# Partial sums over 3, 4 and 6 channel blocks, eight output tiles evacuated by ScalarE, and a new order of the first and fourth token groups

## What is computed

```python
ek = exp(min(k, 30)); ekv = ek * v
nf, df = scan(a * decay + ekv), scan(b * decay + ek)      # forward in time, per channel
nb, db = the same, backward in time
num = nf + nb - ekv + exp(min(u + k, 30)) * v             # den likewise, without v
y = sigmoid(r) * num / max(den, 1e-8) * (0.8 + 0.2 * tf)
h = silu(y @ rw1.T + rb1); logits = (h @ rw2.T + rb2)[:, :16] + gates
coeff = softmax of the two largest logits, 0 elsewhere
base = y @ W.T + bias
xa = einsum('ni,eri->ner', y, A)                          # 16 experts x rank 16 = 256 columns
out = x + base + einsum('ner,eor->no', xa * coeff, B)
```

## Time and profile before

| | us |
|---|---|
| median of 3 runs | 674.62 (674.05 to 674.89) |
| the profiled execution | 672.5 |
| its span | 670.7 |
| TensorE busy, in the span | 593.9 (89%) |
| VectorE busy | 517.5 (77%) |
| ScalarE busy | 360.1 (54%) |
| GpSimd busy | 367.8 (55%) |

### The profile page before, as it was taken

The page is one execution under the profiler, slowest core; times in us unless marked ns, Lnnn a source line. Parts: engine busy times, 40 slices in busy tenths (PEclk is TensorE's granted clock), DMA queues, the critical chain, the costliest instruction groups (busy, mean ns, idle before and its releaser), DMA issues.

```text
span 670.7 us, 6900 instructions
## 1 busy us (share of the span) xinstructions
PE 593.9 (89%) x2554; PEld 478.4 (71%) x2554; DVE 517.5 (77%) x579; ACT 360.1 (54%) x429; POOL 367.8 (55%) x182
## 2 busy tenths in 40 slices
PE   0153689979999989999999959999999999999997
PEld 0142567758878757888778848888788888888786
DVE  7999999999999999999699989999699322031202
ACT  6788899855854676566456584558455220020100
POOL 1799999868857864666266764585347301000100
PEclk9967789989999999999999979999999999999999
DMA  5324467525755811237231622345231502050112
GB/s 196 125 92 155 145 231 235 165 92 124 191 125 111 232 66 63 95 105 243 78 121 52 216 98 78 110 139 175 79 110 48 156 1 90 5 158 0 34 61 79
DMA packets 33249, 78.45 MB, mean 117 GB/s; under 512 B 4736, under 2 KB 4928, under 8 KB 33216
## 3 DMA queue, kind: packets, MB, share of 16 engines
q1 hardware_dynamic: 30912, 73.82, 33.6%
q0 software_dynamic: 2304, 4.20, 4.2%
HBM read 57.03 MB, written 20.97 MB: 116 GB/s over the span
## 4 chain that ended last, share of the span: by engine, by line
PE 64%; DVE 18%; POOL 6%; ACT 5%; issue 4%; DMA 2%; SPq 0%; DVEq 0%; ACTq 0%; POOLq 0%
PE acc L983 20%; PE acc L984 19%; PE acc L985 19%; DVE mix L769 3%; DVE mix L773 3%; DVE mix L778 3%; DVE mix L800 2%; PE acc L1014 2%; DVE eu L788 2%; PE acc L1015 2%; DVE yr L807 1%; DVE mix L756 1%; PE acc L1052 1%; POOL y_lo L679 1%; DVE xo L821 1%
## 5 line engine op out<-in xcount | busy, mean ns | idle before, releaser
L983 PE MATMUL acc<-y_hi,wa_hi 128*128 128x512 f32 x638 | 258.5, 405 | 54.1 <-POOL y_lo L679 49.3
L984 PE MATMUL acc<-y_lo,wa_hi 128*128 128x512 f32 x638 | 254.3, 399 | 0.0
L985 PE MATMUL acc<-y_hi,wa_lo 128*128 128x512 f32 x638 | 254.0, 398 | 0.0
L983 PEld LDWEIGHTS acc<-y_hi,wa_hi 128*128 128x128 f32 x638 | 123.7, 194 | 86.4 <-POOL y_lo L679 50.7
L985 PEld LDWEIGHTS acc<-y_hi,wa_lo 128*128 128x128 f32 x638 | 123.2, 193 | 26.7
L984 PEld LDWEIGHTS acc<-y_lo,wa_hi 128*128 128x128 f32 x638 | 123.9, 194 | 25.2
L669 POOL TENSOR_TENSOR mix<-mix,kv 128x1024 f32<-128x1024 f32 x30 | 71.9, 2396 | 77.8 <-DVE mix L756 77.8
L821 DVE SCALAR_TENSOR_TENSOR xo<-acc,bias_sb,xo 128x512 f32<-128x512 f32 x64 | 46.8, 735 | 73.9 <-PE acc L985 73.7
L679 POOL TENSOR_TENSOR y_lo<-yr,y_hi 128x1024 fp32r<-128x1024 f32 x31 | 76.4, 2464 | 37.5 <-ACT y_hi L428 37.5
L692 POOL TENSOR_TENSOR wx_lo<-xa,wx_hi 128x512 fp32r<-128x512 f32 x16 | 21.2, 1346 | 119.6 <-ACT wx_hi L516 119.6
L650 POOL TENSOR_TENSOR yr<-mix,yr 128x1024 f32<-128x1024 f32 x31 | 74.2, 2394 | 4.9 <-DVE yr L807 2.7
(11 more groups left out here) (126 smaller groups left out, 702.1 us busy)
## 6 DMA issues: line engine op xcount, KB each, us to landing
...
out<-xo SPq DMA_DIRECT2D x64, 256.0 KB, 3.8
xo<-x_cm SPq DMA_DIRECT2D x64, 256.0 KB, 3.8
out<-xo POOLq DMA_DIRECT2D x16, 256.0 KB, 6.2
...
```

What stands on the lines that cost most here:

```text
L983: nc.tensor.matmul(out_ap, wh, yh, start=start, stop=False)
L984: nc.tensor.matmul(out_ap, wh, yl, start=False, stop=False)
L985: return nc.tensor.matmul(out_ap, wl, yh, start=False, stop=stop)
```

## The change

**Depth.** `part_depth` gives tiles 0 to 4 partial sums over 3 units, tiles 5 to 9 over 4 and tiles 10 to 15 over 6. `base` of groups 0 and 1 does what is left: 5 units for tiles 0 to 4, 4 for tiles 5 to 9, 2 for tiles 10 to 15. The places of `drain_part` move with it.

**Evacuation.** Of groups 0 and 1, tiles j = 4 to 7 are evacuated by ScalarE (`drain`, PSUM plus bias, no x). The x that is missing there is added to `out` by four DMAs from DRAM to DRAM, 512 KB each (`add_x`), issued by GpSimd.

**Order.** In group 0 the base products of tile 0 over units 3 to 6 stand ahead of the wait for unit 7, and tile 2's stand ahead of `turn`. In group 3 `turn` comes ahead of all of tile 2, and VectorE's `routing` and `weigh` come later in its step. In group 4 `low_rank` of units 5 and 6 stands ahead of the wait for unit 7 of its batch (unit 23), and half of tile 1 ahead of `logits`. In group 1 `routing` and `weigh` come earlier. The high and low parts of the last weight chunk (12) come a step earlier or ahead in their step.

```diff
-        part_steps = {4: (0, 0, 2), 5: (2, 5, 7), 6: (7, 10, 12), 7: (12, 15, 16)}
-        def base_from(G):
-            return HALF if G < SPLIT else 0
+        part_steps = {4: (0, 2, 5), 5: (5, 7, 10), 6: (10, 12, 13), 7: (13, 15, 16)}
+        part_depth = [HALF - 1] * 5 + [HALF] * 5 + [HALF + 2] * 6
+        def base_from(G, j=0):
+            return part_depth[G * CB + j] if G < SPLIT else 0
...
-        evacs_at = {(CB + 2, AFTER_FWD): (0, 2), (CB + 2, AFTER_FWD_NUM): (2, 4), (CB + 2, AFTER_BWD_DEN): (4, 5),
+        evacs_at = {(CB + 2, AFTER_RATIO): (0, 2), (CB + 2, AFTER_FWD): (2, 4), (CB + 5, AFTER_FWD): (8, 11),
...
+        drains_at = {(CB + 2, AFTER_EXP_K): (4, 6), (CB + 2, AFTER_INVERSE): (6, 7), (CB + 3, AFTER_HI): (7, 8),
+                     (CB + 5, AFTER_EXP_K): (12, 13), (CB + 5, AFTER_INVERSE): (13, 14), (CB + 6, AFTER_HI): (14, 16)}
+        x_adds_at = {(CB, AFTER_LO): (4, 5), (CB + 1, AFTER_GATE): (5, 6), (CB + 2, AFTER_GATE): (6, 7),
+                     (CB + 2, AFTER_LO): (7, 8)}
...
-        routing_at |= {(first_step(G) + 1, AFTER_FWD_NUM): G for G in (1, 3)}
+        routing_at |= {(first_step(3) + 1, AFTER_BWD_DEN): 3}
...
-        weigh_at |= {(first_step(1) + 1, AFTER_P2): 1, (THIRD, AFTER_BWD_DEN): SPLIT, (first_step(3) + 1, AFTER_BWD_DEN): 3}
+        weigh_at |= {(first_step(1) + 1, AFTER_BWD_DEN): 1, (THIRD, AFTER_BWD_DEN): SPLIT, (first_step(3) + 1, AFTER_SCALE): 3}
...
+            def drain(e):
+                G, j = divmod(e, CB)
+                act.wait_ge(out_done, e + 1)
+                if e < XBUF:
+                    act.wait_ge(part_stored[(e - 2) % PBUF], 16 * (PARTS // PBUF))
+                else:
+                    act.wait_ge(out_added[e % XBUF], 16 * (e // XBUF))
+                nc.scalar.activation(xo[:, e % XBUF, :], acc[:, out_bank(G, j), :], ACT.Identity,
+                                     bias=bias_sb[:, j:j + 1]).then_inc(drained, 1)
...
+            def add_x(j):
+                pool.wait_ge(part_stored[j % PBUF], 16 * ((j + CB) // PBUF + 1))
+                nc.gpsimd.dma_start(out[j], x_cm[j], accum_op=ALU.add,
+                                    max_dma_last_dim=4 * T).then_inc(x_added[j - CB // 2], 16)
...
             for p in range(5, PARTS):
                 pe.wait_ge(part_out, p - 4)
-                for kc in range(HALF):
+                for kc in range(part_depth[p]):
+                    if kc >= part_depth[p - 1]:
+                        unit_in(0, kc)
+                        pe.wait_ge(w_lo_ready, base_chunk[kc] + 1)
                     base_part(p, kc)
...
-                        if kc - LAG >= k0:
-                            if kc - LAG == k0:
-                                bank_in(G, 3)
-                                pe.wait_ge(w_lo_ready, base_chunk[CB - 1] + 1)
-                            base(G, 0, kc - LAG)
-                    for kc in range(CB - LAG, CB):
-                        base(G, 0, kc)
+                        if kc == CB - 2:
+                            bank_in(G, 3)
+                            pe.wait_ge(w_lo_ready, base_chunk[CB - 1] + 1)
+                            for k in range(k0, CB - 1):
+                                base(G, 0, k)
+                    base(G, 0, CB - 1)
...
+                        if G == 4:
+                            for a in range(2):
+                                low_rank(G, a, kc)
                     for a in range(2):
-                        for kc in range(first, CB):
+                        for kc in range(CB if G == 4 else first, CB):
                             low_rank(G, a, kc)
...
+                if G == 4:
+                    bank_in(G, 4)
+                    for kc in range(4):
+                        base(G, 1, kc)
                 if G != 1:
                     logits(G)
...
-                ahead = {0: CB, SPLIT: CB - 1, 3: 3}.get(G, k0)
+                ahead = {0: CB - 1, SPLIT: CB - 1}.get(G, k2)
```

More of the change, by code:

```diff
@@ L213, in quarter, with drained_by_act, evacuations, x_loads_to @@
             return tasks_at.get(s, (-1, -1))
+        def drained_by_act(e):
+            return e < PARTS and e % CB >= CB // 2
+        def evacuations(e):
+            return sum(1 for i in range(e + 1) if drained_by_act(i) == drained_by_act(e))
+        def x_loads_to(e):
+            return sum(1 for i in range(e + 1) if not drained_by_act(i) and i % XBUF == e % XBUF)
         def held(g):
@@ L233, in decay_mix_with_routed_lora_channel_major @@
         part_out = sem("part_out")
+        x_added = [sem(f"x_added{j}") for j in range(CB // 2)]
+        drained = sem("drained")
         out_added = [sem(f"out_added{i}") for i in range(XBUF)]
@@ L400, in _ @@
                     load_x(e)
+            for j in range(CB // 2):
+                sp.wait_ge(x_added[j], 16)
             for i in range(XBUF):
@@ L579, in _ @@
                     scale_end_den(s)
-                if routed and G != 4:
+                if routed and G not in (3, 4):
                     exp_gap(G)
@@ L598, in _ @@
                         drain_part(p)
-                if routed:
+                if routed and G not in (0, 3):
                     split_wx(G)
@@ L718, in _ @@
                     split_wx(SPLIT)
+                for j in tiles(x_adds_at, s, AFTER_GATE):
+                    add_x(j)
                 for e in tiles(adds_at, s, AFTER_GATE):
@@ L724, in _ @@
                     split_lo(s - 1)
+                for j in tiles(x_adds_at, s, AFTER_LO):
+                    add_x(j)
                 for e in tiles(adds_at, s, AFTER_LO):
@@ L728, in _ @@
                     weights_lo(n)
-                if q == 1 and G != SPLIT:
+                if q == 1 and G not in (SPLIT, 3):
                     split_wx(G)
@@ L732, in _ @@
                     p1(s + 1)
+                if q == 1 and G == 3:
+                    split_wx(G)
                 if s == CB - 2:
@@ L1078, in unit_in @@
                     pe.wait_ge(lo_ready, g + 1)
-            for kc in range(HALF):
+            for kc in range(part_depth[0]):
                 unit_in(0, kc)
@@ L1187, in _ @@
                     pe.wait_ge(wx_ready, 2 * G + a + 1)
-                    for kc in range(k0, k0 + first):
+                    for kc in depths(G, 3 + a)[:first]:
                         base(G, 3 + a, kc)
@@ L1195, in _ @@
                 for j in range(3, 5):
-                    for kc in range(k0 + first, k0 + 4):
+                    for kc in depths(G, j)[first:]:
                         base(G, j, kc)
```

71 lines of the change are left out of this document (44 added, 27 removed).

## The result

The changed kernel takes **679.25 us** (median of 6 runs, 678.56 to 679.59) where the kernel before took 673.95 in the same comparison (672.86 to 674.89). That is 5.3 us more; the ratio, which is formed from the runs beside each other, is **1.0077** (95% interval 1.0064 to 1.0090). The forecast was 677.2 (+2.6 us), in the range 670.5 to 681.5. The direction and most of the mechanism held; the loss is twice the size.

A forecast was written before the change was run, and what follows sets the result against it. TensorE and VectorE were taken to bound different stages, with no TensorE idle time behind its wait for unit 23. +9.3 us before unit 15 and -6.7 behind it gave +2.6, from 674.62 to 677.2 us, range 670.5 to 681.5.

The forecast's parts named there:

- what the deep sums do first: Unit 5 to `hidden(0)`: TensorE waits some 9 us for unit 5, VectorE 7.6 at `inverse(6)`; `hidden` shifts by +13.1 us.
- from `hid` to `weigh(0)`: Group 0: a 3.5 us wait at `logits`, more matmuls and a clock restart add +1.5 us (0.5 to 2.8).
- Other parts of this stretch cost nothing that I can see.: Before unit 15: four `add_x` take GpSimd about 1 us each, within its idle time, so no cost.
- rival of the accumulating DMAs: Steps 10 and 11: ScalarE's `drain(6)` waits for an `add_x` to land, costing VectorE 3 to 4 us: 681; chance 0.15.
- a sign of being wrong: Steps 10 and 11: a ScalarE wait on `out<-xo` of over 2 us would show the forecast wrong.
- the wait for `logits(1)`: Group 1: VectorE reaches `routing(1)` at 197.0, TensorE starts `logits(1)` at 199.0; VectorE waits 3.0 us.
- The gains of 5.5 and 2.8: Before unit 15: eight evacuations leave VectorE, -5.5 us; its waits on TensorE at 195 to 215 us go, -2.8.
- group 3: Behind unit 15: later routing and earlier `turn` remove VectorE's wait at `weigh`, making VectorE and unit 23 4.3 us earlier.
- group 4: Around unit 23: TensorE's wait goes, `logits(4)` at 396.8, `turn` at 401.7, -7.1 us; the term taken was -6.7 (-5.0 to -8.3).
- the first stretch: Everything before unit 15: 14.6 - 5.5 - 2.8 + 3.0 makes unit 15 later by +9.3 us (6 to 11.5).
- Mostly absorbed: TensorE keeps full clock after the waits, `hid` of group 0 ends before 137.5: 671.8 us; chance of faster 0.31.
- Both halves cancel: `weigh(0)` late by 13.0 and the rest as forecast: sum within a us of zero, 675; chance 0.16.

The follow-up runs named there:

- e2_depth_only: The kernel before with only the partial sums over 3, 4 and 6 units and their copies' new places: 686.12 us, ratio 1.0178.
- e8_depth5: The changed kernel with partial sums over 3, 4 and 5 units instead of 3, 4 and 6: 670.50 us, ratio 0.9950.
- e6_g0_old: The changed kernel with all partial sums over four units and group 0's TensorE order of the kernel before: 665.52 us, ratio 0.9877.
- e5_adds_early: The changed kernel with the four `add_x` moved from steps 8, 9 and 10 to steps 8 and 9: 676.16 us, ratio 1.0035.
- e9_best: The changed kernel with all partial sums over four units, group 0's old TensorE order and the early `add_x`: 662.95 us, ratio 0.9837.
- e4_late_copies: The changed kernel with ScalarE's copies of partial sums 10 and 11 moved behind `inverse(6)`: 679.64 us, ratio 1.0084.
- e11_g0_old_deep: The changed kernel, sums over 3, 4 and 6 units kept, with group 0's TensorE order of the kernel before: 675.85 us, ratio 1.0053.

## Why the prediction was right and where it was short

**Right: what the deep sums do first.** The step from unit 5 to `hidden(0)` came out nearly row by row. Unit 5's low part: forecast 100.0, measured 100.80 (98.45 + 2.35). TensorE's wait: 9, measured 9.56. `inverse(6)`: 108.2, measured 109.04. VectorE at `ratio(6)`: 7.6, measured 7.7. Start of group 0: 123.8, measured 124.68. End of `hid`: 139.8, measured 140.7. e2_depth_only shows that this alone costs 12 us, and e8_depth5 that it depends on the one unit.

**Short: from `hid` to `weigh(0)`.** Forecast +1.5 behind a shift of +13.1, so +14.6; measured +2.2 (16.1 less 13.9, since `hidden(0)` went from 127.43 to 141.36). The wait at `logits` was forecast at 3.5 and is 3.58; the restart of the clock, which I had put between nothing and 2.7 us, came with eight matmuls at half clock (147.29 to 150.34), at 0.2 us more each 1.6 us, in the upper half of that bound. The 9 to 12 matmuls that group 0's new order puts ahead of `hid` were in the sum, but I had not seen them as a part of the change that loses by itself; e6_g0_old shows that it does.

**Wrong: "Other parts of this stretch cost nothing that I can see."** That is the step that failed. The four `add_x` were costed at their issue time, about 1 us each, and they do take 0.83 to 1.08 us. But with three transfers under way GpSimd stood 4.67 us, and VectorE 2.47 us for `p1(11)`. e5_adds_early puts the price at 0.42% (2.8 us). My rival of the accumulating DMAs looked at the right transfers and the wrong engine: ScalarE did wait for one (2.11 us at 182.48, behind an `add_out` that landed at 182.40), which is over the 2 us that I had named as a sign of being wrong; VectorE was at that time waiting for `p1(11)` until 184.69, so it lay in the shadow of GpSimd's stop.

**Mis-sized: the wait for `logits(1)`.** Forecast 3.0 us. TensorE came at 199.83 (forecast 199.0), but VectorE came only at 201.90 (forecast 197.0): 2.5 of the 4.9 us are its wait at `p1(11)`, 1.5 the later `weigh(0)`, and 0.9 are not assigned. In place of the 3.0 there is a wait of 1.0 us for ScalarE's exponential at L915. Taken together: forecast 14.6 - 5.5 - 2.8 + 3.0 = 9.3. With the measured terms it is 16.1 - 5.5 - 2.8 + 2.5 + 1.0 = 11.3, against 12.0 measured; 0.7 us are not assigned. The gains of 5.5 and 2.8 held: VectorE is busy 5.5 us less, and the two waits of the earlier trace rows are gone. In e5_adds_early, without the stop, unit 15 is late by 9.2, all but the forecast; that is luck in part, since there `weigh(0)` is late by 16.6 and not 14.6, and the wait for `logits(1)` is 1.1 and not 3.0.

**Right: group 3.** The lateness of 11.9 behind unit 15 taken off, the backward scan starts at 322.8 (forecast 322.8), `turn` at 329.0 after 0.79 (329.0 after 0.9), `weigh(3)` at 332.1 (332.1) and the scan behind it at 333.3 (333.3). VectorE is 4.2 us earlier at unit 20, forecast 4.3.

**Short: group 4.** TensorE doesn't wait for unit 23, `logits(4)` is at 396.8 (forecast 396.8) and `turn(4)` at 402.3 (401.7), 0.4 us of it since the routing took 4.3 us in place of 3.9, with a wait of 0.33 for ScalarE's exponential in it. What was left out is the step behind it. `spread` needs ScalarE's copy of the turned coefficients (`cat_t`), and in ScalarE's list this copy stands behind a scaled column that waits for VectorE's first scan behind the routing. VectorE, ScalarE and TensorE of the kernel before, and then VectorE and ScalarE of the changed one:

```profile
407.20 2.28 DVE L769 TENSOR_TENSOR_SCAN mix<-d_ps,mix 128x1024 f32<-128x1024 f32 x1
409.51 0.29 ACT L440 ACTIVATE mix<-mix,rdelta_g 128x1 f32<-128x1 f32 x1 [4.87 <-DVE mix L769]
410.67 0.58 ACT L511 ACTIVATE cat_t<-acc 64x512 fp32r<-64x512 f32 x1
411.29 0.50 PE L1067 MATMUL acc<-cat_t,expand_r 32*128 32x512 f32 x2
```

```profile
414.06 2.28 DVE L824 TENSOR_TENSOR_SCAN mix<-d_ps,mix 128x1024 f32<-128x1024 f32 x1
416.37 0.29 ACT L457 ACTIVATE mix<-mix,rdelta_g 128x1 f32<-128x1 f32 x1 [4.43 <-DVE mix L824]
417.52 0.57 ACT L528 ACTIVATE cat_t<-acc 64x512 fp32r<-64x512 f32 x1
```

`spread` starts 4.09 us behind that scan before the change and 4.08 behind it after (418.14). Nine matmuls stand between `turn` and `spread` in both kernels. Before, TensorE came to `turn` 1.6 us after the routing's end and to `spread` just as the copy was done, so no wait showed; now it comes to `turn` as the routing ends and waits 1.36 us at `spread`. The forecast of -7.1 followed TensorE's shorter list as far as `turn`. From there on only VectorE's shift counts, 414.06 - 407.20 - 11.9 = -5.0. In the forecast's terms, with 0.6 at `turn` and 1.4 at `spread`, it is -5.1, and measured is 6.9 - 12.0 = -5.1. The term was -6.7 on record.

**The sum.** +9.3 was +12.0 and -6.7 was -5.1: +6.9 in the trace, +5.3 by the medians (the profiled execution of the kernel before, 672.5, is 1.5 us under its median, that of the changed kernel is at its own). Of the difference of 4.3 us in the trace the first stretch has 2.7, about what taking GpSimd's stop away gives back (2.8).

**The rivals.** "Mostly absorbed" falls: `hid` ended at 140.7, far behind its point of decision of 137.5, and TensorE did run at half clock. The granted clock in a window of the changed kernel behind the wait (columns: window, length, PE, PEld, DVE, ACT, POOL, granted clock, DMA share, GB/s) and in the same window of e9_best:

```profile
100.00:105.00 5.00, 4.15 (x10) 3.28 (x11) 3.60 (x3) 0.59 (x1) 4.37 (x4) 0.50 0.73 247
```

```profile
100.00:105.00 5.00, 5.00 (x24) 4.14 (x23) 4.86 (x5) 4.64 (x7) 4.37 (x4) 1.00 0.86 249
```

Without the wait TensorE has its full clock and starts 24 matmuls instead of 10. Twelve starts behind 100.85 (101.44 to 106.13) are 0.43 us apart, which at 0.2 us more each is 2.4 us, near the 2.7 of the earlier trace rows. By the Trainium skill (TensorE: Matmul & The Clock Gate, "What's actually happening") the number of slow matmuls at a kernel's start varies between runs, 6, 11 or 14. The traces agree for a restart: the changed kernel has 8 to 12 in each of its eight stretches at half clock, and behind the wait for unit 5, where it has 12, e4_late_copies has 6, e5_adds_early 5 and e11_g0_old_deep 13. "Both halves cancel" falls with the 16.1 at `weigh(0)`.
